# Last sequence's output product and norm of a 16-head attention carried over into the following stream, and the stream's first splits made ahead of it

## The reference

```python
    x = L0_attn_a_x
    x = x + _L0_attn_a_ref(_layernorm(x, axis=-1), L0_attn_a_w_qkv, L0_attn_a_b_qkv, L0_attn_a_w_proj, L0_attn_a_b_proj)
    x = x + _L0_ffn_ref(_layernorm(x, axis=-1), L0_ffn_wqkv, ...)
    x = x + _L0_attn_b_ref(_layernorm(x, axis=-1), L0_attn_b_Wq, ...)
    x = x + _L0_ffn_ref(_layernorm(x, axis=-1), L0_ffn_wqkv, ...)
    return x
```

## Time and profile before

| | us |
|---|---|
| runs | 1087.09, 1094.47, 1099.30 |
| median of the runs | 1094.47 |
| the profiled execution, its device time | 1097.6 |
| the profiled execution, its span from first to last instruction | 1095.5 |
| PE busy in that span | 998.4 |
| DVE busy | 737.7 |
| ACT busy | 738.7 |
| POOL busy | 387.1 |

### The profile page before, as it was taken

The page is one execution under the profiler, slowest core; times in us unless marked ns, Lnnn a source line. Parts: engine busy times, 40 slices in busy tenths (PEclk is TensorE's granted clock), DMA queues, the critical chain, the costliest instruction groups (busy, mean ns, idle before and its releaser), DMA issues.

```text
span 1095.5 us, 21794 instructions
## 1 busy us (share of the span) xinstructions
PE 998.4 (91%) x8208; PEld 594.3 (54%) x8208; DVE 737.7 (67%) x1202; ACT 738.7 (67%) x1565; POOL 387.1 (35%) x270
## 2 busy tenths in 40 slices
PE   6799999999957899999999898998989999999986
PEld 3332333322325667667666666666666766766752
DVE  3656676565439777868777667667767777877651
ACT  2345677565837787777787667676768788787762
POOL 2100113000118545445454343334335544544410
PEclk9756898675989999999999999999999999999997
DMA  2200000000013101101010000000001101011100
GB/s 67 61 13 1 2 1 1 2 1 1 1 30 93 26 16 31 26 17 31 19 23 21 15 21 16 21 15 21 16 10 27 31 16 26 21 26 35 31 20 12
DMA packets 25219, 23.66 MB, mean 22 GB/s; under 512 B 10610, under 2 KB 17052, under 8 KB 25116
## 3 DMA queue, kind: packets, MB, share of 16 engines
q1 hardware_dynamic: 25116, 22.27, 8.7%
HBM read 6.16 MB, written 1.05 MB: 7 GB/s over the span
## 4 chain that ended last, share of the span: by engine, by line
PE 60%; DVE 7%; issue 2%; ACT 1%; POOL 1%; DVEq 0%; POOLq 0%
PE psum L1215 8%; PE psum L1187 5%; PE psum L1127 5%; PE psum L1089 5%; PE psum L1099 5%; PE psum L1148 5%; PE psum L1137 4%; PE psum L1091 4%; PE psum L1090 4%; PE psum L1223 4%; PE psum L1160 3%; PE psum L1208 2%; PE psum L1202 2%; PE psum L1112 2%; DVE f_PT L1467 2%
## 5 line engine op out<-in xcount | busy, mean ns | idle before, releaser
L1018 POOL TENSOR_TENSOR f_A<-f_A,f_BS 128x1024 f32<-128x1024 f32 x64 | 151.0, 2360 | 226.0 <-DVE f_BS L1450 225.4
L729 DVE TENSOR_REDUCE a_M<-psum 128x2 f32<-128x1024 f32 x128 | 154.2, 1220 | 77.4 <-PE psum L534 76.7
L661 ACT ACTIVATE a_PT<-psum 128x1024 f32<-128x1024 f32 x128 | 129.6, 1023 | 83.9 <-PE psum L544 82.2
L1023 POOL TENSOR_TENSOR f_A<-f_A,f_RN 128x1024 f32<-128x1024 f32 x64 | 121.7, 1902 | 91.1 <-ACT f_RN L1336 87.2
L1321 ACT ACTIVATE f_PW<-psum,f_NM 128x128 f32<-128x128 f32 x512 | 138.1, 380 | 4.2 <-DVE f_NM L1475 4.2
L1287 ACT ACTIVATE f_SQ<-psum 128x512 f32<-128x512 f32 x128 | 75.2, 607 | 76.6 <-PE psum L1091 72.3
L1475 DVE TENSOR_REDUCE f_NM<-psum 128x4 f32<-128x512 f32 x128 | 82.3, 684 | 65.8 <-PE psum L1127 64.7
L1446 DVE TENSOR_TENSOR f_A<-psum,cos 128x512 f32<-128x512 f32 x128 | 87.7, 685 | 39.3 <-ACT f_SQ L1287 39.2
L1148 PE MATMUL psum<-f_VS,f_PT 128*64 128x65 f32 x1024 | 80.7, 227 | 33.5 <-DVE f_PT L1467 14.5
L1148 PEld LDWEIGHTS psum<-f_VS,f_PT 128*64 128x64 f32 x1024 | 67.4, 138 | 66.5 <-issue 48.4
L472 PE MATMUL psum<-a_PT,a_VA 128*12 128x512 f32 x512 | 92.3, 806 | 1.6 <-ACT a_PT L661 1.3
(11 more groups left out here) (175 smaller groups left out, 2000.0 us busy)
## 6 DMA issues: line engine op xcount, KB each, us to landing
f_VS<-f_V SPq DMA_DIRECT2D x112, 130.0 KB, 2.3
raw<-L_ffn_wqkv_dram SPq DMA_DIRECT2D x2, 768.0 KB, 5.3
a_XT<-L_attn_a_x_dram SPq DMA_DIRECT2D x4, 256.0 KB, 2.9
a_QS<-a_MROW SPq DMA_DIRECT2D x64, 2.0 KB, 1.7
out_dram<-f_OUT SPq DMA_DIRECT2D x4, 256.0 KB, 2.3
f_w<-L_ffn_w_dram SPq DMA_DIRECT2D x2, 341.0 KB
tables<-const_dram SPq DMA_DIRECT2D x1, 512.0 KB, 3.9
f_wo<-L_ffn_wo_dram SPq DMA_DIRECT2D x8, 64.0 KB
```

The lines of the kernel that those rows point to most:

```text
L661: nc.scalar.activation(PT[:, h:h + 2, t, :], psum[:, pair("by_key", i), :], ACT.Exp, scale=float(DA) ** -0.5).then_inc(s("exped"), 1)
L729: nc.vector.tensor_reduce(M[:, quads % 2, t, 2 * j:2 * j + 2], psum[:, pair("scores", i), :], AX_X, ALU.max).then_inc(s("maxed"), 1)
L1018: nc.gpsimd.tensor_tensor(A[:, k % 2, :, :], A[:, k % 2, :, :], BS[:, k % 2, :, :], ALU.add)\
L1023: nc.gpsimd.tensor_tensor(x, x, RN[:, k % 2, :, None].to_broadcast([P, 2 * HW, DW]), ALU.mult)\
```

## The change

In `attention_a` the last sequence loses `features`, `project`, `center_y` and `var_y` (`CARRIED`). Its divided sums `OT` now live outside the phase, and the stream makes the closing work: `features_a` (PE and ACT) at step 0, `project_a` at step 1, and the norm as `center_a` and `var_a` at step 2, with Y written by DVE (L1513 in the code before) in place of POOL.

The lead of sequence 0 moves to slot 130 of `attention_a`, on DVE. Since the attention still runs there, `HH` and `HL` also become outer tensors, and the attention uses them: `HH` for its own high and low parts of queries and keys, `HL` as one of the two halves of `KS`. The leads of sequences 1, 2 and 3 now stand at steps 1, 3 and 8 (`of_lead`).

```diff
+        g.HH = sb("HH", [P, SEQS, T], F32R)
+        g.HL = sb("HL", [P, SEQS, T], F32R)
+        g.OT = sb("OT", [P, 4, HA, DA])
...
+        if slot == SEQS * SLOTS + 2:
+            plan.append(("lead", 0))
...
+                if n == SEQS - 1 and work in CARRIED:
+                    continue
...
+CARRIED = ("features", "project", "center_y", "var_y")
...
-        QH = sb("QH", [P, 2, T], F32R)
-        QL = sb("QL", [P, 2, T], F32R)
...
-        KS = sb("KS", [P, 2, QUADS, T], F32R)
+        QH, QL = g.HH[:, 0:2, :], g.HH[:, 2:4, :]
+        KS = (g.HL, sb("KS", [P, QUADS, T], F32R))
+        OT = g.OT
...
-                pool.wait_ge(s("y_new"), SEQS)
+                pool.wait_ge(s("y_new"), SEQS - 1)
...
+                    elif work == "lead":
+                        dve.wait_ge(s("k_stack"), SEQS * QUADS)
+                        dve.wait_ge(s("scored_by_key"), (SEQS - 1) * SLOTS)
+                        dve.wait_ge(s("y_new"), 1)
+                        nc.vector.memset(zero[64:P, :], 0.0).then_inc(s("lead_zero"), 1)
+                        dve.wait_ge(s("lead_zero"), 1)
+                        for part in (g.HH, g.HL):
+                            nc.vector.tensor_copy(part[64:P, :, 0], zero[64:P, :]).then_inc(s("first_tokens"), 1)
+                        dve.wait_ge(s("first_tokens"), 2)
+                        for rows, to, of in SHIFTED:
+                            nc.vector.tensor_copy(g.HH[rows, 0, to], Y[rows, 0, of]).then_inc(s("lead_high"), 1)
+                        dve.wait_ge(s("lead_high"), 2)
+                        for rows, to, of in SHIFTED:
+                            nc.vector.tensor_tensor(g.HL[rows, 0, to], Y[rows, 0, of],
+                                                    g.HH[rows, 0, to].bitcast(F32), ALU.subtract)\
+                              .then_inc(s("lead_low"), 1)
...
+                dve.wait_ge(s("lead_low"), 2)
+                dve.wait_ge(s("divided"), SEQS * QUADS)
...
+def of_lead(k):
+
+    return {1: 1, 3: 2, 8: 3}.get(k)
+
+
+def of_first(k):
+
+    return SEQS - 1 if k == 0 else None
...
-    "PE": [("latent", 8, of_sequence), ("features_b", 10, of_sequence),
+    "PE": [("features_a", 0, of_first), ("project_a", 1, of_first), ("latent", 8, of_sequence),
+           ("features_b", 10, of_sequence),
...
+    "DVE": [("lead", 0, of_lead), ("project_a", 1, of_first), ("latent", 8, of_sequence), ("rope", 0, of_tile), ("context", 9, of_sequence), ("project_b", 10, of_sequence),
...
+                    elif stage == "features_a":
+                        dst = take("features_a", i)
+                        for t in range(4):
+                            last = nc.tensor.transpose(dst[:, P * t:P * t + P],
+                                                       g.OT[:, t, :, :].rearrange("p h d -> p (h d)"), g.ident)
+                        last.then_inc(s("features_a"), 1)
+                    elif stage == "project_a":
+                        pe.wait_ge(s("o_ready_a"), 1)
+                        nc.tensor.matmul(take("project_a", i), g.wpa[:, :], OF[:, :], start=True, stop=True)\
+                          .then_inc(s("project_a"), 1)
...
+                    elif stage == "features_a":
+                        act.wait_ge(s("features_a"), 1)
+                        nc.scalar.activation(OF[:, :], psum[:, bank("features_a", i), :], ACT.Identity,
+                                             bias=g.bqk[:, 2:3]).then_inc(s("o_ready_a"), 1)
...
                     elif stage == "lead":
+                        if i == SEQS - 1:
+                            dve.wait_ge(s("ln_used"), number["a", i] + 1)
                         lead(i)
+                    elif stage == "project_a":
+                        dve.wait_ge(s("project_a"), 1)
+                        nc.vector.scalar_tensor_tensor(out=X[:, i, :], in0=psum[:, bank("project_a", i), :],
+                                                       scalar=g.bpa[:, 0:1], in1=X[:, i, :],
+                                                       op0=ALU.add, op1=ALU.add).then_inc(s("x_added"), 1)
```

More of the change, by code:

```diff
@@ L273, in attention_a @@
             singles += [("sums_done", i)]
-        elif work not in ("scores", "by_key", "sums1", "sums2", "stats"):
+        elif work not in ("scores", "by_key", "sums1", "sums2", "stats", "lead"):
             singles += [(work, i)]
@@ L534, in _ @@
                             last = nc.tensor.matmul(dst[:, h, :], QS[rows, n % 2, quads % QUADS, P * t:P * t + P],
-                                                    KS[rows, n % 2, quads % QUADS, :], start=True, stop=True)
+                                                    KS[n % 2][rows, quads % QUADS, :], start=True, stop=True)
                         last.then_inc(s("scored"), 1)
@@ L543, in _ @@
                             rows = slice(32 * (2 * j + h), 32 * (2 * j + h) + ROWS_E)
-                            last = nc.tensor.matmul(dst[:, h, :], KS[rows, n % 2, quads % QUADS, P * t:P * t + P],
+                            last = nc.tensor.matmul(dst[:, h, :], KS[n % 2][rows, quads % QUADS, P * t:P * t + P],
                                                     QS[rows, n % 2, quads % QUADS, :], start=True, stop=True)
@@ L810 @@
-    "DVE": [("lead", 0, of_tile), ("latent", 8, of_sequence), ("rope", 0, of_tile), ("context", 9, of_sequence), ("project_b", 10, of_sequence),
+           ("center_mlp", 4, of_group), ("center_a", 2, of_first), ("center_b", 7, of_sequence),
+           ("center_y", 10, of_sequence), ("keys_b", 8, of_sequence), ("tokens_b", 9, of_sequence), ("scores", 1, of_tile),
+           ("var_mlp", 4, of_group), ("var_a", 2, of_first), ("var_b", 7, of_sequence),
+           ("var_y", 10, of_sequence), ("turn_p_2", 2, of_tile), ("w2", 6, of_group), ("wo", 3, of_group), ("sums", 2, of_tile), ("store", 6, of_end)],
@@ new lines @@
+    "ACT": [("features_a", 0, of_first), ("latent", 8, of_sequence), ("features_b", 10, of_sequence),
+            ("squares", 0, of_tile), ("turn", 1, of_tile), ("values", 0, of_tile), ("turn_o", 3, of_tile),
+            ("center_mlp", 4, of_group), ("center_a", 2, of_first), ("center_b", 7, of_sequence),
+            ("center_y", 10, of_sequence), ("split", SEQS, of_tile), ("w1", 5, of_group), ("turn_p", 2, of_tile), ("keys_b", 8, of_sequence),
+            ("norm", 0, of_tile), ("var_mlp", 4, of_group), ("var_a", 2, of_first), ("var_b", 7, of_sequence),
+            ("var_y", 10, of_sequence), ("soften", 1, of_tile), ("store", 6, of_end)],
@@ L814 @@
             ("w2", 6, of_group), ("sums", 2, of_tile)],
-    "POOL": [("lead", 0, of_tile), ("split", SEQS, of_tile), ("scale", 0, of_tile), ("w2", 6, of_group),
+    "POOL": [("lead", 0, of_lead), ("split", SEQS, of_tile), ("scale", 0, of_tile), ("w2", 6, of_group),
              ("wo", 3, of_group), ("latent", 8, of_sequence), ("var_y", 10, of_sequence)],
@@ L826, in engine_plan @@
             if 0 <= k < TOTAL and whose(k) is not None:
-                if stage == "lead" and not 1 <= k < SEQS or stage == "split" and k >= 3:
+                if stage == "split" and k >= 3:
                     continue
@@ L1025, in _ @@
                     elif stage == "lead":
-                        pool.wait_ge(s("lead_high"), i + 1)
-                        low_part(i, "lead_shifted", 2 * i)
+                        pool.wait_ge(s("lead_high"), i)
+                        low_part(i, "lead_shifted", 2 * (i - 1))
                     elif stage == "split":
@@ L1198, in _ @@
                             x = X[:, j, :]
+                        elif use == "a":
+                            pe.wait_ge(s("x_added"), 1)
+                            x = X[:, j, :]
                         else:
@@ L1425, in lead @@
                     last.then_inc(s("lead_high"), 1)
-                nc.vector.memset(LR[64:P, 0:SEQS], 0.0).then_inc(s("lead_zero"), 1)
-                dve.wait_ge(s("lead_zero"), 1)
-                for part in (HH, HL):
-                    nc.vector.tensor_copy(part[64:P, :, 0], LR[64:P, 0:SEQS]).then_inc(s("first_tokens"), 1)
-                dve.wait_ge(s("first_tokens"), 2)
-                lead(0)
-                dve.wait_ge(s("lead_high"), 1)
-                for rows, to, of in SHIFTED:
-                    nc.vector.tensor_tensor(HL[rows, 0, to], Y[rows, 0, of], HH[rows, 0, to].bitcast(F32),
-                                            ALU.subtract).then_inc(s("lead_shifted"), 1)
                 for stage, i in engine_plan("DVE"):
```

27 lines of the change are left out of this document (9 added, 18 removed).

## The result

| | before | after |
|---|---|---|
| median of 18 runs each | 1089.72 | 1077.34 |
| lowest to highest | 1084.86 to 1100.21 | 1074.48 to 1091.35 |
| ratio, with its 95% interval | | 0.9876 [0.9847, 0.9904] |
| the profiled execution, its span | 1095.5 | 1089.4 |
| end of the attention's last division in it | 309.22 | 314.35 |

The ratio stands for -13.5 us, [-16.7, -10.5], of 1089.72; forecast were -11.5. The kernel is faster by a little over 1%. The ratio is that of the mean times without the slow run of 1091.35, which is also the profiled one and whose attention ran longer at the lower clock. The medians alone differ by 12.4, the lowest runs by 10.4. Because the attention's length varies so much, I compare distances from the end of the last division, in which the two profiles differ by 11.2.

A forecast was written before the change was run, and what follows sets the result against it. It took one-engine-at-a-time chains at the passage into the stream, then a DVE and ACT loop, as the bound. -9.19 - 4.50 + 0.75 + 1.4 + 0 = -11.5 took 1094.5 to 1083.0 us, range 1073 to 1092.

The forecast's parts named there:

- The tail: From the attention's last division to the stream's first operation: the closing chain leaves, the 1.46 gap stays; -9.19 us.
- Lead in slot 130: In the attention on DVE: the lead of sequence 0 takes 3.1 of 3.99 us of idleness, so costs 0.
- The head: Stream start to step 0's sum of squares: 5.12 us instead of 9.62, so -4.50 at full clock, -3.43 at the lower.
- Step 1: On DVE between the casts and `rope(1)`: the sum into X is added; +0.75 us.
- Bound by a loop through DVE and ACT: First steps of the stream: DVE hardly ever idles there, so DVE and ACT, not PE, set the pace; no size.
- Step 2: The stream's step 2 gains the norm, on the loop, and loses a pair of casts; +1.4 us, bounds -0.3 to +4.3.
- Steps 3 and 8: Casts of other sequences there: a like pair replaced at step 3, idle time covering step 8; 0, uncovered 1.2 us.
- a cast that does meet POOL: Rival: moved casts at step 3 or 8 start during a POOL pass and pay 2.7 us; result -8.8, chance 0.08.
- the shifted values: Rival: in the stream their transfer lands late, margin shrinking to 1.2 us; result about -10.5, chance 0.07.
- neither hidden nor in full on the loop: Two rivals on step 2's norm: hidden, result -13.2, chance 0.10; in full on the loop, +4.3, result -8.6, chance 0.14.
- From step 4 on ... the shift is carried to the end: Rest of the stream: orders and bank rotation stay as before, so the gain reaches the end unchanged; 0.
- slower rival: PE's clock drops at the new passage and stays at 1.2 GHz into PE-bound stream; +2.2 us, chance 0.03.

The follow-up runs named there:

- three leads in the tail: The changed kernel with the leads of sequences 0, 1 and 2 all in tail slots of the attention; step 1's sum of squares came 2.99 us earlier, no ratio given.
- the lead alone: The kernel before with the lead of sequence 0 moved to slot 130, closing work left in the attention; ratio 0.9956 [0.9907, 1.0005].
- before, again: The kernel before, unaltered, profiled a second time; 786.32 us from the last division to the end.
- `w1_last` early: The changed kernel with the third block of the MLP's hidden layer on DVE ahead of `tokens_b`; ratio 0.9789 [0.9704, 0.9873].

## Why the prediction was right in part, and which of its steps failed

The forecast of -11.5 lies in the measured interval, and the trace has -11.2 and -10.4 from the last division on. But it came out of two errors that nearly cancel: the first steps cost 1.1 less than forecast (at mark 4, -12.66 against -11.54), and the rest of the stream 1.4 to 2.2 more. That the sum came out is luck.

- *The tail*, -9.19: right, -9.14 (a gap of 1.51 instead of 1.46).
- *Lead in slot 130*, 0: right; 1.26 us of waiting are left.
- *The head*, -4.50: -4.71. Squares started 1.88 after the stream's start (forecast 1.97), right behind OF. "I take full clock" was half right: full for the first three products, until 317.08, then 1.2 GHz (0.63 a product there), so that the second squares waited 0.27 for PE. The chain on ACT and DVE hid most of it.
- *Step 1*, +0.75: right, 0.68 by the marks. By the rule that I cited from the Trainium skill ("SBUF — State Buffer", "Who interferes with whom") the sum into X doesn't contend with POOL; the trace agrees: in the kernel with three leads in the tail it lies wholly under POOL's first pass and takes 0.74.
- *"Bound by a loop through DVE and ACT"*: only in part. Three leads in the tail take 4.7 us of casts off DVE in steps 1 and 3, and mark 4 comes 0.60 earlier.
- *Step 2*, "+1.4": the term that was mis-sized; the norm costs 0.62 and the removed casts give 0.1, so +0.5. In the prediction's chain the first product of the norm pushed the scores by its full 1.12. They moved by 0.68 against mark 1: the product holds PE for 0.95 (334.89 to 335.84), as 1.12 is a modelled end, and part of that lies in the wait for ACT's copies of the turned tile. The second product starts before the modelled end of the scores, so the exponentials come 1.25 later and not 1.85. rope(3) came 27.88 after the last division, 0.9 ahead of the forecast (338.0 less 309.22).
- *Steps 3 and 8*, 0: right in what is left. The casts take 0.85 each; those of step 8 put mark 8 back by 0.57, and mark 9 has 0.52 of it again. The rivals fell: a cast that does meet POOL at step 2 costs 0.03 at mark 4, the sums waited for DVE's copies and not for the shifted values, the norm was neither hidden nor in full on the loop.
- *"From step 4 on ... the shift is carried to the end"*: this step failed. From mark 4 to the end the change takes 1.4 and 2.2 us longer than before. Of it 0.5 goes by mark 28, about 0.02 a step, in the lead alone too; what makes it was not tried. The largest part, 1.5 to 2.1, is PE's clock in four late steps, where the granted clock is as low as 0.83 and work that only fills PE's wait brings it to 1.00. The other steps up to mark 63 take 0.2 to 0.3 more, and the profile with the smaller loss has the 1.5 back behind mark 63. The prediction looked at the orders and the banks from step 4 on and put the clock there at nothing, since the slices of the stream in the earlier trace rows stand at 9; a slice of 27.4 us is too coarse for a fall of some us. Its slower rival had the right mechanism in the wrong place and size.
- *1083.0*: 5.7 above the measured median, of which 4.7 are the starting point: the three runs shown had a median of 1094.47, the eighteen 1089.72. The range held.

What stays open is the rest between -13.5 timed and -11 in the traces. It may be chance, as the interval reaches to -10.5, or lie ahead of the last division, where one kernel's profiles differ by 8.5 us (314.35 and 305.83); two profiles of before against twelve show no shift of the attention, but do not exclude 2 us. The lowest runs differ by 10.4 (1084.86 and 1074.48), which is what the traces give. That points to the number of executions in which the attention runs long, and whether the change alters that number no run here shows.

## What to carry to other kernels

Compare two profiles by distances from an event behind the noisy stretch: here the stream repeats to hundredths of a us as far as mark 28, behind that to about one us, and the attention to some ten us. A saving ahead of a long pipeline is not simply carried through it: wherever PE waits some us, look at the granted clock of the work behind the wait, for a shift of half a us elsewhere can move the fall onto other products. What helped here was to split that wait or to fill it: one line moved in DVE's order brought 3.5 to 4.4 us and the filling 3 to 4.

## What the runs showed of the hardware

In the four late steps the fall of the clock repeated with the work, although the attention ahead of it did not: before and before, again, whose attentions differ by 4.84 us, have these steps at 19.60, 18.44, 18.47, 18.43 and at 19.60, 18.46, 18.43, 18.46. It does not always repeat so well: the two profiles of the changed kernel, 8.52 us apart, differ by 0.1 to 0.3 in each of these steps (18.82, 19.11, 19.52, 19.60 and 18.73, 18.94, 19.23, 19.51), and by 1.5 behind mark 63. The clock also fell where PE had waited only 1.56 and 1.11 us with 0.7 us of sums between (the 18.43 of `w1_last` early), and in the same code two groups earlier it did not (17.39).
